# A Mamba-2 scan step whose running sum is split inside its PSUM bank, with the work of four engines in a new order

## The chip, the core and the metric

The kernel runs on one core of one Trainium2 chip, as one launch. The metric is the time of the whole launch on the device, in microseconds (us). TensorE (PE in the profile), VectorE (DVE), ScalarE (ACT), GpSimd (POOL) and SyncE (SP) each run their own instructions in the order in which they are written and meet only at semaphores.

## What is computed

The input is x with 8 sequences of 1024 tokens and 256 features. Two Mamba-2 layers are followed by three blocks of a quantised linear network (the MLP part, which the change leaves alone). Cut to what matters here, a layer is:

```python
h = layernorm(h)
z, xBC, dt = split(h @ in_w.T)                 # 512, 640 and 8 columns
dt  = softplus(dt + dt_bias)
xBC = silu(causal_conv(xBC, 4 taps) + conv_b)  # per channel, along the tokens
x, B, C = split(xBC)                           # 8 heads of 64, and 64 states each
state = exp(dt * A) * state + dt * x (x) B     # token by token
y = state @ C + D * x
y = y * silu(z);  y = y * rsqrt(mean(y * y) + eps) * rms_w
h = h + y @ out_w.T
```

The scan over tokens is computed in chunks of 128 tokens. Within a chunk the product of the decays between tokens j and i is exp(-|cum_i - cum_j|), with cum the running sum of dt * A. The kernel needs cum on the free axis as well as on the partitions, so it splits each fp32 value into three bf16 parts, whose sum is the value, and turns and spreads those with bf16 products.

## The kernel before

One *item* is one chunk of 128 tokens of a group of four sequences. There are 8 chunks and 2 groups, so 16 items in a layer and 32 in all. Every engine has a function `step(n, ...)`, written out by hand, that does its share of item n and of the items after it: the scan and the output of item n, the projections, convolution and `dt` of item n+1, and the norm of item n+2. `over_items` calls it 32 times (the middle twelve of a layer are a loop over two steps, the others are written out). Nothing but that order and the semaphores says when something runs. An instruction that waits holds up all that stands behind it on its engine.

The names that the rest needs, by what they do (q is a half of one sequence's heads, 0 to 7; b is a sequence, 0 to 3; t a quarter of the inner width, 0 to 3; i one of five convolved tiles):

- TensorE: `project_conv(i)`, `project_z(t)` and `project_dt`, six products each (L382, L369); `turn_dt`, `turn_x(b)`, `turn_b`, `turn_u`, transposes; `sum_da`, the running sums, into `front[0]` (L400); `turn_cum`, which transposes the split sum (L408); `decays(q)` (L437); `carry(b)` (L470); `outputs(t)` (L487, L493); `new_state(s)` (L480); `scores` (L425); `result(s)`, the output projection (L530); `square_sums` (L519).
- ScalarE: `raw_conv(i)` moves a projected tile to `xpad` (L658); `silu_conv(i)` (L671); `double_c` issues two DMAs from ScalarE's own queue (L678); `norm`, four instructions (L624); `softplus` (L644 to L648); `exp_decay(q)`, an Abs and an Exp (L696, L698); `exp_carry(b)` (L707); `silu_z(t)` (L692); `square(t)` (L711); `keep_b` (L703).
- GpSimd: `first_tap(i)` (L860), `to_end(b)` (L869), `decay_state` (L876), `layer_norm`, a power (L812) and a product (L824), `gate(t)` (L852), `norm_residual` (L843, L846; in the first layer only), `add_squares` (L837), `second_operands` (L830).
- VectorE: `convolve(i, 0..2)` (L1067, L1070, L1073), which accumulates in the PSUM bank of the projection; `split_sums` (L1005, L1011, L1014); `skip(t)` (L1100); `scale_x(b)` (L1090); `scale_c(b)` (L1095); `weigh(q)` (L1085); `finish(s)` (L1126); `layer_moments`; `decay_operands` (L1033), `first_operands` (L1039), `add_state` (L1110).

A convolved tile passes four engines: `project_conv(i)`, `raw_conv(i)`, `first_tap(i)`, and `convolve(i, 0)` to `convolve(i, 2)`. `turn_cum` waits for the last step of the fifth tile, because it writes the PSUM bank `front[1]` that this tile has used, and for the end of `split_sums`. `turn_u` waits for `silu_z(3)`, which reads the same bank, and `silu_z(3)` waits for `gate(3)`, which reads the buffer that it writes.

Of the kernel before, what the change touches and what calls it, by code (L numbers as in the profile page):

```python
# [174 lines left out]
def mamba_layers(nc, x, h, out, w):  # L175

    with ExitStack() as ctx:
# [49 lines left out]
        rest1, rest2 = sb("rest1", [P, NB, NH]), sb("rest2", [P, NB, NH])  # L227
# [107 lines left out]
        def _(pe):  # L335
# [223 lines left out]
            def step(n, layer, c, p):  # L559
                more, more2 = follows(n, 1), follows(n, 2)  # L560
                decays(n, 4)
                if more:
                    project_conv(n + 1, 0)
                    turn_dt(n + 1)
                if follows_any(n):
# [20 lines left out]
                new_state(n, 0)  # L586
                outputs(n, p, 1)
                if more:
                    project_conv(n + 1, 4)
                    sum_da(n + 1)  # L590
                new_state(n, 1)
                outputs(n, p, 2)
                outputs(n, p, 3)
                if more:
# [5 lines left out]
                    scores(n + 1, 1 - p)  # L600
                    decays(n + 1, 0)
                    decays(n + 1, 1)
                if more2:
                    turn_u(n + 2, p)
# [15 lines left out]
        def _(act):  # L620
# [123 lines left out]
            def step(n, layer, c, p):  # L744
                more, more2 = follows(n, 1), follows(n, 2)
                layer1 = layer_of(n, layer, 1)
                if more:
                    keep_dt(n + 1)
                    raw_conv(n + 1, layer1, 1 - p, 0)
                exp_decay(n, 3)  # L750
# [5 lines left out]
                if more:  # L756
                    raw_conv(n + 1, layer1, 1 - p, 2)
# [3 lines left out]
                exp_decay(n, 7)  # L761
                exp_carry(n, 2)
                exp_carry(n, 3)
                if more:
                    raw_conv(n + 1, layer1, 1 - p, 3)
                    softplus(n + 1)
# [3 lines left out]
                if more:  # L770
# [7 lines left out]
                if more:  # L778
                    keep_halo(n + 1, 1 - p)
                    silu_conv(n + 1, layer1, 1 - p, 3)  # L780
                    silu_conv(n + 1, layer1, 1 - p, 4)
# [1016 lines left out]
```

## Time and profile before

| | us |
|---|---|
| three runs, median (lowest to highest) | 2013.32 (2010.97 to 2015.57) |
| the profiled execution | 2011.51 |
| its span in the profile | 2009.7 |

| engine | busy us | share of the span |
|---|---|---|
| TensorE | 1819.0 | 91% |
| VectorE | 1565.4 | 78% |
| ScalarE | 1258.7 | 63% |
| GpSimd | 1195.9 | 60% |

The launch falls into a ramp of about 100 us, the 16 items of the first layer, the 16 of the second, and from about 1515 us on the MLP part. An item takes about 45 us. The timeline rows give the start of an instruction from the start of the span, its duration, engine, line, operation and tiles, and in brackets how long the engine had been idle before it and who released it. Neighbouring instructions overlap a little, so that the distance of two starts is what an instruction really costs its engine: 0.66 us on VectorE for one shown as 0.75.

### The profile page before, as it was taken

What the parts mean: (1) busy time and instruction counts of PE and PEld (TensorE: products, weight loads), DVE (VectorE), ACT (ScalarE), POOL (GpSimd) and SP (SyncE); (2) the same over time, 40 slices, a digit from 0 to 9 for tenths busy, and PEclk for the clock granted to TensorE, in tenths of its full rate; (3) what the DMA queues carried; (4) which work ended last, traced back from release to release, by engine and by line L of the source; (5) the groups of instructions that cost most, each with busy time, mean ns of one, the idle gap of its engine ahead of it and who ended that gap; (6) DMA issues with size and microseconds to landing.
All of it is one profiled execution on the core that took longest, in us unless ns stands there. A gap on an engine that the chain in (4) does not pass through costs nothing. (4 is left out here: it accounts for less than half of the span.)

```text
span 2009.7 us, 36493 instructions
## 1 busy us (share of the span) xinstructions
PE 1819.0 (91%) x12544; PEld 1366.7 (68%) x12544; DVE 1565.4 (78%) x3311; ACT 1258.7 (63%) x2221; POOL 1195.9 (60%) x1032
## 2 busy tenths in 40 slices
PE   4899999999999999999999999999985698889898
PEld 3566676666676667766676776766764577777776
DVE  4677788887787776877777777777744799999986
ACT  3667666776666776667777676667740355555555
POOL 2466666666666654555555555555550586878785
PEclk9899999999999999999999999999996799999999
DMA  4011111111111111111111111111004201102001
GB/s 139 22 38 38 38 37 39 55 48 37 42 37 37 37 38 38 38 45 59 40 41 37 37 37 37 37 49 45 27 17 146 84 1 62 65 32 95 32 12 43
DMA packets 87271, 91.96 MB, mean 46 GB/s; under 512 B 4928, under 2 KB 82448, under 8 KB 87184
## 3 DMA queue, kind: packets, MB, share of 16 engines
q1 hardware_dynamic: 79360, 79.46, 12.2%
q10 hardware_dynamic: 7824, 11.37, 2.3%
q8 instruction: 51, 0.84, 0.2%
q14 instruction: 36, 0.29, 0.0%
HBM read 57.26 MB, written 25.17 MB: 41 GB/s over the span
## 5 line engine op out<-in xcount | busy, mean ns | idle before, releaser
L860 POOL TENSOR_TENSOR L_xc<-L_xpad,L_vec 128x512 f32<-128x512 f32 x160 | 166.1, 1038 | 318.1 <-ACT L_xpad L658 318.1
L852 POOL TENSOR_TENSOR L_yg<-L_yg,L_sz 128x512 f32<-128x512 f32 x128 | 165.4, 1292 | 159.5 <-DVE L_yg L1100 158.2
L382 PE MATMUL L_front<-L_uhi,L_whi 128*128 128x512 f32 x576 | 250.1, 434 | 9.5 <-DVE L_xc L1073 6.2
L1085 DVE TENSOR_TENSOR L_m<-L_dbank,L_gm 128x512 f32<-128x512 f32 x256 | 173.4, 688 | 101.8 <-ACT L_dbank L698 101.8
L530 PE MATMUL L_mix<-L_wo,L_yg 128*128 128x256 f32 x1024 | 235.4, 384 | 2.6 <-POOL L_yg L852 2.6
L382 PE MATMUL L_front<-L_uhi,L_wlo 128*128 128x512 f32 x576 | 229.2, 398 | 0.0
L382 PE MATMUL L_front<-L_ulo,L_whi 128*128 128x512 f32 x576 | 228.7, 397 | 0.0
L530 PEld LDWEIGHTS L_mix<-L_wo,L_yg 128*128 128x128 f32 x1024 | 191.9, 192 | 27.7 <-POOL L_yg L852 2.8
L658 ACT ACTIVATE L_xpad<-L_front,L_pbias 128x512 f32<-128x512 f32 x160 | 110.1, 688 | 153.1 <-PE L_front L382 153.1
L487 PE MATMUL L_ybank<-L_m,L_dtx 128*64 128x128 f32 x2048 | 158.1, 280 | 33.1 <-DVE L_yg L1100 25.6
L696 ACT ACTIVATE L_dbank<-L_dbank 128x512 f32<-128x512 f32 x256 | 148.7, 581 | 49.7 <-PE L_dbank L437 48.0
L1614 POOL TENSOR_TENSOR M_alo<-M_hT,M_ahi 128x512 fp32r<-128x512 f32 x96 | 125.4, 1310 | 75.0 <-DVE M_ahi L1676 75.0
L487 PEld LDWEIGHTS L_ybank<-L_m,L_dtx 128*64 128x64 f32 x2048 | 113.7, 136 | 81.5 <-issue 33.9
L493 PE MATMUL L_ybank<-L_cs,L_state 64*64 64x128 f32 x2048 | 160.5, 280 | 0.0
L698 ACT ACTIVATE L_dbank<-L_dbank 128x512 f32<-128x512 f32 x256 | 149.0, 582 | 7.5
L382 PEld LDWEIGHTS L_front<-L_uhi,L_whi 128*128 128x128 f32 x576 | 109.6, 190 | 55.3 <-DVE L_xc L1073 20.5
L692 ACT ACTIVATE L_sz<-L_front,L_pbias 128x512 f32<-128x512 f32 x128 | 88.2, 689 | 90.1 <-PE L_front L382 58.7
L1565 ACT ACTIVATE M_g<-M_lin,M_beta,M_gamma 128x512 f32<-128x512 f32 x96 | 73.9, 770 | 111.5 <-PE M_lin L1500 111.5
L869 POOL TENSOR_TENSOR L_wx<-L_dtx,L_decay 128x512 f32<-128x512 f32 x128 | 132.1, 1043 | 8.1 <-DVE L_dtx L1090 7.1
L1621 POOL TENSOR_TENSOR M_alo<-M_g,M_ahi 128x512 fp32r<-128x512 f32 x96 | 134.3, 1418 | 4.2 <-ACT M_ahi L1573 4.1
L1067 DVE SCALAR_TENSOR_TENSOR L_front<-L_front,L_vec,L_xc 128x512 f32<-128x512 f32 x160 | 120.4, 752 | 19.4 <-POOL L_xc L860 19.3
L493 PEld LDWEIGHTS L_ybank<-L_cs,L_state 64*64 64x64 f32 x2048 | 106.4, 132 | 38.4 <-issue 38.4
(176 smaller groups left out, 4949.3 us busy)
## 6 DMA issues: line engine op xcount, KB each, us to landing
h<-L_hres SPq DMA_DIRECT2D x32, 512.0 KB, 3.0
L_hin<-in_x SPq DMA_DIRECT2D x16, 512.0 KB, 4.7
L_hres<-in_x SPq DMA_DIRECT2D x16, 512.0 KB, 3.9
L_cc<-L_xc ACTq DMA_DIRECT2D x64, 128.0 KB, 2.3
L_hin<-h SPq DMA_DIRECT2D x16, 512.0 KB, 4.7
L_hres<-h SPq DMA_DIRECT2D x16, 512.0 KB, 3.8
M_hin<-h SPq DMA_DIRECT2D x16, 512.0 KB, 7.1
M_xin<-in_x SPq DMA_DIRECT2D x16, 512.0 KB, 7.1
```

Source lines behind the costliest of these rows:

```text
L382: last = nc.tensor.matmul(to[:, :], ww[:, kd, tile * P:(tile + 1) * P], a[:, kd, :], start=i == 0, stop=i == len(passes) - 1)
L487: nc.tensor.matmul(ybank[t % 2][half, b * P:(b + 1) * P], dtx[:, b, 2 * t + odd, :], m[:, b, 2 * t + odd, :], start=b == 0, stop=False, sk ...
L493: made = nc.tensor.matmul(ybank[t % 2][half, b * P:(b + 1) * P], state[p][half, b, t, :], cs[half, b, t, :], start=False, stop=True, skip_ ...
L530: last = nc.tensor.matmul(mix[1 - s][:, (b % 2) * DM:(b % 2 + 1) * DM], yg[:, t, b * P:(b + 1) * P], wo[layer][:, t, :], start=t == 0, sto ...
L696: nc.scalar.activation(dbank[q % 2][:, :], dbank[q % 2][:, :], ACT.Abs).then_inc(d_abs, 1)
L698: nc.scalar.activation(dbank[q % 2][:, :], dbank[q % 2][:, :], ACT.Exp, scale=-1.0).then_inc(d_exp, 1)
L852: nc.gpsimd.tensor_tensor(yg[:, t, :], yg[:, t, :], sz[:, t, :], ALU.mult).then_inc(y_gated, 1)
L860: nc.gpsimd.tensor_tensor(xc[p][:, q, :].rearrange("p (b i) -> p b i", b=NB), xpad[:, q, :, 0:P], vector(layer, "conv_w", q * TAPS, 1).uns ...
L869: nc.gpsimd.tensor_tensor(wx[:, b, :, :], dtx[:, b, :, :], decay[p][:, b, :].unsqueeze(2).broadcast_to([P, NH, HD]), ALU.mult).then_inc(wx ...
L1085: nc.vector.tensor_tensor(m[:, b, 4 * half:4 * half + 4, :], dbank[half][:, :].rearrange("p (h i) -> p h i", i=P), gm[:, b, :].unsqueeze(1 ...
L1614: nc.gpsimd.tensor_tensor(alo[u][:, kd, :], hT[u][:, kd, :], ahi[u][:, kd, :].bitcast(F32), ALU.subtract).then_inc(h_lo, 1)
L1621: nc.gpsimd.tensor_tensor(alo[u][:, kd, :], g[u][:, kd, :], ahi[u][:, kd, :].bitcast(F32), ALU.subtract).then_inc(g_lo, 1)
```

## The change

`split_sums` no longer reads the copy of the sums in SBUF. It casts and subtracts from the PSUM bank in which TensorE has left them, and puts the two remainders beside them in that bank (`rest1` and `rest2` in SBUF are gone). The copy to SBUF stays, for ScalarE. The split doesn't wait for it any more, and `project_z(0)`, which overwrites the bank, waits for the end of the split too.

```diff
 def project_z(n, t):
     if t == 0:
         pe.wait_ge(sums_out, n + 1)
+        pe.wait_ge(split, 5 * n + 5)
...
-cum = sums[:, 0, :, :]
-dve.wait_ge(sums_out, n + 1)
+def beside(i):
+    at = (PARTS + i) * NB * NH
+    return front[0][:, at:at + NB * NH].rearrange("p (b h) -> p b h", b=NB)
+
+cum = front[0][:, 0:NB * NH].rearrange("p (b h) -> p b h", b=NB)
+rest1, rest2 = beside(0), beside(1)
 part(0, cum)
```

The rest is order. The products of TensorE are the same ones. Its step begins:

```diff
 # TensorE, step
+project_conv(n + 1, 0)
+turn_x(n, p, 0)
+turn_dt(n + 1)
 decays(n, 4)
-project_conv(n + 1, 0)
-turn_dt(n + 1)
 result(n - 1, layer_of(n, layer, -1), 1)
 project_conv(n + 1, 1)
-turn_x(n, p, 0)
 turn_x(n, p, 1)
+turn_x(n, p, 2)
 decays(n, 5)
 decays(n, 6)
-turn_x(n, p, 2)
 turn_x(n, p, 3)
...
 outputs(n, p, 0)
-new_state(n, 0)
 outputs(n, p, 1)
+outputs(n, p, 2)
 project_conv(n + 1, 4)
 sum_da(n + 1)
+new_state(n, 0)
 new_state(n, 1)
-outputs(n, p, 2)
 outputs(n, p, 3)
```

and further down the first two `decays` of the next item stand ahead of `scores`. On GpSimd:

```diff
 # GpSimd, step
+decay_state(n, p)
 first_tap(n + 1, layer1, 1 - p, 0)
 first_tap(n + 1, layer1, 1 - p, 1)
 to_end(n, p, 0)
-decay_state(n, p)
+first_tap(n + 1, layer1, 1 - p, 2)
 to_end(n, p, 1)
+first_tap(n + 1, layer1, 1 - p, 3)
+layer_norm(n + 2)
 to_end(n, p, 2)
...
+to_end(n, p, 3)
 gate(n, 0)
-to_end(n, p, 3)
-layer_norm(n + 2)
 first_tap(n + 1, layer1, 1 - p, 4)
 gate(n, 1)
```

and `second_operands` stands behind the three `add_squares`. On ScalarE `raw_conv(2)` moves from ahead of `keep_b` to behind `exp_decay(7)`, `softplus` ahead of `raw_conv(3)`, and further down:

```diff
 # ScalarE, step
 silu_conv(n + 1, layer1, 1 - p, 0)
-silu_conv(n + 1, layer1, 1 - p, 1)
-square(n, 0)
-raw_conv(n + 1, layer1, 1 - p, 4)
-double_c(n + 1, 1 - p)
 norm(n + 2, p)
+silu_conv(n + 1, layer1, 1 - p, 1)
+double_c(n + 1, 1 - p)
 silu_conv(n + 1, layer1, 1 - p, 2)
+raw_conv(n + 1, layer1, 1 - p, 4)
+square(n, 0)
 square(n, 1)
+square(n, 2)
```

On VectorE, among others, `scale_x(0)` comes before the convolution of the first tile, `scale_x(2)` and `scale_x(3)` one place earlier each, `finish_dt` behind `skip(0)`, and `skip(1)`, `skip(2)` and `skip(3)` are moved.

How the instructions stand on VectorE around the split, before:

```order
L1073 SCALAR_TENSOR_TENSOR L_xc<-L_xpad,L_vec,L_front 128x512
L99 REGISTER_ALU
L1005 COPY L_sums<-L_front 128x96
L1011 CAST L_cum<-L_sums 128x4x2x8
L1014 TENSOR_TENSOR L_rest<-L_sums,L_cum 128x32
L1011 CAST L_cum<-L_rest 128x4x2x8
L1014 TENSOR_TENSOR L_rest<-L_rest,L_cum 128x32
L1011 CAST L_cum<-L_rest 128x4x2x8
L1066 REGISTER_ALU
L1067 SCALAR_TENSOR_TENSOR L_front<-L_front,L_vec,L_xc 128x512
L1100 SCALAR_TENSOR_TENSOR L_yg<-L_xc,L_vec,L_ybank 128x512
```

and of the changed kernel, whose line numbers are up to five higher:

```order
L1078 SCALAR_TENSOR_TENSOR L_xc<-L_xpad,L_vec,L_front 128x512
L1105 SCALAR_TENSOR_TENSOR L_yg<-L_xc,L_vec,L_ybank 128x512
L99 REGISTER_ALU
L1006 COPY L_sums<-L_front 128x96
L1012 CAST L_cum<-L_front 128x4x2x8
L1015 TENSOR_TENSOR L_front<-L_front,L_cum 128x32
L1012 CAST L_cum<-L_front 128x4x2x8
L1015 TENSOR_TENSOR L_front<-L_front,L_cum 128x32
L1012 CAST L_cum<-L_front 128x4x2x8
L1071 REGISTER_ALU
L1072 SCALAR_TENSOR_TENSOR L_front<-L_front,L_vec,L_xc 128x512
L1105 SCALAR_TENSOR_TENSOR L_yg<-L_xc,L_vec,L_ybank 128x512
```

The casts and remainders read and write `L_front` in place of `L_sums` and `L_rest`, and `skip(1)` (L1100, now L1105) has moved from behind the split to ahead of it.

ScalarE around the move of the fifth convolved tile (L658), the two DMAs (L678) and the norm (L624), before:

```order
L711 ACTIVATE L_sq<-L_yg 128x512
L652 REGISTER_ALU
L658 ACTIVATE L_xpad<-L_front,L_pbias 128x4x128
L674 ISA
L99 REGISTER_ALU
L678 DMA L_cc<-L_xc 64x512 x2
L622 REGISTER_ALU
L624 ACTIVATE L_hin<-L_hin,L_shift,L_rstd 128x256 x4
L670 REGISTER_ALU
L671 ACTIVATE L_xc<-L_xc,L_cbias 128x512
```

and of the changed kernel, from `silu_conv(0)` on:

```order
L672 ACTIVATE L_xc<-L_xc,L_cbias 128x512
L623 REGISTER_ALU
L625 ACTIVATE L_hin<-L_hin,L_shift,L_rstd 128x256 x4
L671 REGISTER_ALU
L672 ACTIVATE L_xc<-L_xc,L_cbias 128x512
L675 ISA
L99 REGISTER_ALU
L679 DMA L_cc<-L_xc 64x512 x2
L671 REGISTER_ALU
L672 ACTIVATE L_xc<-L_xc,L_cbias 128x512
L653 REGISTER_ALU
L659 ACTIVATE L_xpad<-L_front,L_pbias 128x4x128
```

The norm, both DMAs and one more `silu_conv` now stand ahead of `raw_conv(4)`, where it was ahead of all three.

## Rows read from the trace of the kernel before

**Rows 1.** The page, busy time, share of the span and instructions of each engine.
```profile
PE 1819.0 (91%) x12544; PEld 1366.7 (68%) x12544; DVE 1565.4 (78%) x3311; ACT 1258.7 (63%) x2221; POOL 1195.9 (60%) x1032
```

**Rows 2.** Timeline of VectorE, L1115, once per item: items 2, 12, 19, 30.
```profile
203.89 0.16 DVE L1115 TENSOR_SCALAR L_ssq<-L_ybank 128x4 f32<-128x4 f32 x1 [0.27 <-PE L_ybank L519]
...
659.77 0.16 DVE L1115 TENSOR_SCALAR L_ssq<-L_ybank 128x4 f32<-128x4 f32 x1 [0.27 <-PE L_ybank L519]
...
937.50 0.16 DVE L1115 TENSOR_SCALAR L_ssq<-L_ybank 128x4 f32<-128x4 f32 x1 [0.72 <-PE L_ybank L519]
...
1431.65 0.16 DVE L1115 TENSOR_SCALAR L_ssq<-L_ybank 128x4 f32<-128x4 f32 x1 [0.72 <-PE L_ybank L519]
```

**Rows 3.** Timeline of TensorE over one item of the first layer.
```profile
607.99 1.09 PE L342 MATMUL L_front<-L_kept,L_hin 128*128 128x128 f32 x8 [0.59 <-ACT L_sz L692]
...
615.43 0.39 PE L437 MATMUL L_dbank<-L_dmov,L_dstat 64*128 64x512 bf16 x1
...
620.95 0.58 PE L382 MATMUL L_front<-L_uhi,L_whi 128*128 128x512 f32 x1
...
622.54 0.60 PE L450 MATMUL L_mix<-L_kept,L_xc 128*128 128x128 f32 x4
623.82 0.66 PE L450 MATMUL L_mix<-L_kept,L_xc 128*128 128x128 f32 x4 [0.69 <-DVE L_hres L1126]
...
630.70 0.73 PE L470 MATMUL L_mix<-L_dmov,L_sel 64*128 64x512 bf16 x4
631.77 0.44 PE L487 MATMUL L_ybank<-L_m,L_dtx 128*64 128x128 f32 x4 [0.34 <-DVE L_m L1085]
...
643.54 1.09 PE L487 MATMUL L_ybank<-L_m,L_dtx 128*64 128x128 f32 x16 [0.76 <-DVE L_yg L1100]
...
645.60 0.28 PE L408 MATMUL L_front<-L_identb,L_cum 128*128 128x128 bf16 x2
```

**Rows 4.** The same view, `turn_u` of an item of the second layer.
```profile
1156.13 1.09 PE L342 MATMUL L_front<-L_kept,L_hin 128*128 128x128 f32 x8
```

**Rows 5.** Timeline of ScalarE (ACTq: its queue issuing DMAs), the same item.
```profile
631.34 1.07 ACT L707 ACTIVATE L_mix<-L_mix 128x512 f32<-128x512 f32 x2 [0.65 <-PE L_mix L470]
632.31 0.69 ACT L658 ACTIVATE L_xpad<-L_front,L_pbias 128x512 f32<-128x512 f32 x1
632.88 0.24 ACT L644 ACTIVATE L_dtabs<-L_dtraw 128x32 f32<-128x32 f32 x1
...
634.94 1.28 ACT L671 ACT_TABLE_LOAD   x1
...
639.54 1.12 ACTq L678 DMA_DIRECT2D L_cc<-L_xc  x2
640.77 2.08 ACT L624 ACTIVATE L_hin<-L_hin,L_shift,L_rstd 128x256 f32<-128x256 f32 x4 [0.76 <-POOL L_shift L824]
642.75 0.70 ACT L671 ACTIVATE L_xc<-L_xc,L_cbias 128x512 f32<-128x512 f32 x1
```

**Rows 6.** Timeline of GpSimd, the same item.
```profile
638.86 1.00 POOL L812 TENSOR_TENSOR L_rstd<-L_var,L_power 128x4 f32<-128x4 f32 x1
640.03 0.20 POOL L824 TENSOR_TENSOR L_shift<-L_mom,L_rstd 128x4 f32<-128x4 f32 x1 [0.17 <-POOL L_rstd L812]
640.18 1.04 POOL L860 TENSOR_TENSOR L_xc<-L_xpad,L_vec 128x512 f32<-128x512 f32 x1
```

**Rows 7.** Timeline of VectorE, the same item.
```profile
620.25 0.18 DVE L992 TENSOR_TENSOR L_dtraw<-L_front,L_dtb 128x32 f32<-128x32 f32 x1
...
640.37 0.91 DVE L1011 CAST L_cum<-L_sums 128x64 bf16<-128x64 f32 x1
...
641.53 0.20 DVE L1011 CAST L_cum<-L_rest 128x64 bf16<-128x64 f32 x1
...
642.09 0.75 DVE L1067 SCALAR_TENSOR_TENSOR L_front<-L_front,L_vec,L_xc 128x512 f32<-128x512 f32 x1
642.75 0.74 DVE L1100 SCALAR_TENSOR_TENSOR L_yg<-L_xc,L_vec,L_ybank 128x512 f32<-128x512 f32 x1
```

More of the change, by code:

```diff
@@ L560, in step @@
                 more, more2 = follows(n, 1), follows(n, 2)
-                decays(n, 4)
                 if more:
                     project_conv(n + 1, 0)
+                turn_x(n, p, 0)
+                if more:
                     turn_dt(n + 1)
+                decays(n, 4)
                 if follows_any(n):
@@ L748, in step @@
                     keep_dt(n + 1)
+                exp_decay(n, 3)
+                if more:
                     raw_conv(n + 1, layer1, 1 - p, 0)
-                exp_decay(n, 3)
                 exp_decay(n, 4)
@@ L755, in step @@
                 exp_decay(n, 6)
-                if more:
-                    raw_conv(n + 1, layer1, 1 - p, 2)
                 keep_b(n)
@@ L761, in step @@
                 exp_decay(n, 7)
+                if more:
+                    raw_conv(n + 1, layer1, 1 - p, 2)
                 exp_carry(n, 2)
@@ L775, in step @@
                 if more:
+                    silu_conv(n + 1, layer1, 1 - p, 1)
+                    double_c(n + 1, 1 - p)
                     silu_conv(n + 1, layer1, 1 - p, 2)
+                    raw_conv(n + 1, layer1, 1 - p, 4)
+                square(n, 0)
                 square(n, 1)
[L778 to L781, printed above, removed]
-                    silu_z(n + 1, layer1, 0)
                 square(n, 2)
                 if more:
+                    silu_conv(n + 1, layer1, 1 - p, 3)
+                    silu_z(n + 1, layer1, 0)
+                    keep_halo(n + 1, 1 - p)
                     silu_z(n + 1, layer1, 1)
+                    silu_conv(n + 1, layer1, 1 - p, 4)
                     silu_z(n + 1, layer1, 2)
                     silu_z(n + 1, layer1, 3)
+                    exp_decay(n + 1, 0)
                 square(n, 3)
                 if more:
-                    exp_decay(n + 1, 0)
                     exp_decay(n + 1, 1)
@@ L1169, in step @@
                 if more:
+                    set_halo(n + 1, 1 - p)
+                weigh(n, 3)
+                scale_x(n, p, 0)
+                if more:
+                    bias_dt(n + 1, layer1)
                     convolve(n + 1, layer1, 1 - p, 0, 0)
-                    bias_dt(n + 1, layer1)
-                    convolve(n + 1, layer1, 1 - p, 0, 1)
-                weigh(n, 3)
                 weigh(n, 4)
                 if more:
-                    convolve(n + 1, layer1, 1 - p, 0, 2)
+                    convolve(n + 1, layer1, 1 - p, 0, 1)
                 if follows_any(n):
                     finish(n - 1, layer_of(n, layer, -1), None, 1 - p, 1)
-                scale_x(n, p, 0)
+                if more:
+                    convolve(n + 1, layer1, 1 - p, 0, 2)
                 scale_x(n, p, 1)
+                scale_x(n, p, 2)
                 if more:
                     convolve(n + 1, layer1, 1 - p, 1, 0)
-                scale_x(n, p, 2)
+                scale_x(n, p, 3)
                 if more:
                     convolve(n + 1, layer1, 1 - p, 1, 1)
-                scale_x(n, p, 3)
                 weigh(n, 5)
@@ L1205, in step @@
                     convolve(n + 1, layer1, 1 - p, 3, 2)
+                skip(n, layer, p, 1)
+                if more:
                     split_sums(n + 1)
                     convolve(n + 1, layer1, 1 - p, 4, 0)
-                skip(n, layer, p, 1)
+                skip(n, layer, p, 2)
                 if more:
                     convolve(n + 1, layer1, 1 - p, 4, 1)
-                skip(n, layer, p, 2)
-                if more:
                     convolve(n + 1, layer1, 1 - p, 4, 2)
                     decay_operands(n + 1)
-                skip(n, layer, p, 3)
+                    first_operands(n + 1)
                 add_state(n, p, 0)
-                if more:
-                    first_operands(n + 1)
                 add_state(n, p, 1)
@@ L1221, in step @@
                     clear_halo(n, p)
+                skip(n, layer, p, 3)
                 if more:
```

33 lines of the change are left out of this document (15 added, 18 removed).

## Prediction

> **What bounds the kernel now.** The page gives TensorE 91% of the span [rows 1], so I first ask how often it waits. The change only touches the two layers, so I need the length of an item: one row of VectorE stands once in each. In the first layer ten items lie between 203.89 and 659.77, which is 45.59 us each. In the second, eleven lie between 937.50 and 1431.65, 44.92 us each [rows 2].
>
> The timeline of TensorE over one item then shows where it is idle [rows 3]: 0.59 us before `turn_u` (released by `silu_z(3)`), 0.69 before `turn_x(1)` (`finish`), 0.34 before `outputs(0)` (`weigh(7)`), 0.76 before `outputs(3)` (`skip(1)`). In the second layer the wait before `turn_u` is absent [rows 4], and 45.59 - 44.92 = 0.67 is about its size. So four waits of 2.4 us are shown. With what hides between the products I put the loss at 3 us an item, and TensorE without waits at 42.3 to 42.6. With some 15 items' distance in each layer, all of it is worth at most 30 x 2.8, about 84 us. TensorE's work is unchanged: the change can only bring what its waits lose, and an order is as good as the latest thing that it makes TensorE wait for. The question is which wait takes the place of the four.
>
> **The split.** In the item shown, its first cast takes 0.91 us, the later ones of the same size 0.20 [rows 7]. The long one started at 640.37 and ended at 641.28, while GpSimd ran `first_tap(4)` from 640.18 to 641.22 [rows 6]: it was held until GpSimd was through. A read from PSUM of 128x32 took 0.18 us [rows 7], so the five new steps should be no dearer than the old, and the first loses its wait for the copy too, 0.1 to 0.2 us. The split gets up to 0.8 us shorter, in the ramp once as well.
> The Trainium skill (SBUF — State Buffer, the section on the two sides of SBUF) says that VectorE in a two-port mode and GpSimd hold one pair of ports in turn, and "VectorE: DVE Perf Modes" (why PSUM operands drop a tier) that a PSUM operand excludes that mode. The row of 0.91 us agrees. The same page's cost table speaks against the change: 120 fixed cycles from PSUM in place of 58 from SBUF, which is 5 x 0.065 = 0.3 us more by my estimate. The row of 0.18 us does not show it. With it the split would save 0.5 us, not 0.8.
>
> **The first part of an item, by the new order.** I walk with starts of the old item, whose step begins at 615.43 [rows 3].
> - TensorE. Ahead of `project_conv(1)` now also stands `turn_x(0)`, 0.43 to 0.47 us, and `project_conv(0)` follows `project_dt` 0.1 us sooner. So `project_conv(1)` starts at 620.95 + 0.35 = 621.3 and ends 1.59 later (622.54 - 620.95), at 622.9. `finish` let `turn_x(1)` start at 623.82, so it ran from about 622.9, behind `convolve(0, 2)`. It now stands ahead of that and is done at about 622.8, so the 0.69 us before `turn_x(1)` goes to nearly nothing.
> - The second tile: `raw_conv(1)` 623.1 to 623.8 (0.69 [rows 5]), `first_tap(1)` to 624.9 (1.04 [rows 6]), then on VectorE `convolve(1, 0)`, `scale_x(3)`, `convolve(1, 1)`, `weigh(5)`, `convolve(1, 2)`, at 0.66 a convolution and 0.60 a product, done at 628.2. `project_conv(3)` waits for it: 628.3 to 629.9. `outputs(0)` follows at about 630.7, 1.1 us sooner than before, and its wait of 0.34 shrinks to 0.2.
> - `carry(2)` from 629.9; ScalarE gets it 0.64 later (630.70 to 631.34), so `exp_carry(2)` and `(3)` run 630.5 to 631.5 (0.97 for both).
> - Now the tail on ScalarE. `softplus` costs 634.94 - 632.88 = 2.06: to 633.6. `raw_conv(3)`, now behind it, to 634.2 (0.57 of ScalarE's time, done at 634.3). The table load 1.29 and `silu_conv(0)` 0.66: 636.1. Meanwhile GpSimd: `first_tap(3)` 634.3 to 635.4, then `layer_norm`, 1.37 us from the start of the power to the end of the product (638.86 to 640.23 [rows 6]), shift ready at 636.7. So `norm` starts at 636.8 and takes 1.98 (642.75 - 640.77). `silu_conv(1)` at 638.8. Then `double_c`: its two DMAs block ScalarE's queue, 1.12 us from 639.54 on. The norm behind them started at 640.77, though the shift that the row names was there at 640.23. It was the DMA issue that held it. So from `silu_conv(1)` to `silu_conv(2)` it is 0.22 + 1.12 + 0.11 = 1.45 and not 0.66: 640.2. `raw_conv(4)` 640.9 to 641.6, where it ended at 640.0 before.
> - `first_tap(4)` to 642.7, `convolve(4, 0)`, `skip(2)`, `convolve(4, 1)` at 0.66 a start, `convolve(4, 2)` behind them with 0.13 more for its dependence, done at 645.6. `turn_cum` waits for that.
>
> So `turn_cum` comes at about 645.65, against 645.60 before. TensorE has done all else that stands ahead of it by 643.8: the four waits of before shrink to some 0.4 us, and a new one of 1.8 us stands before `turn_cum`, for the fifth tile. The split ends at about 641.4, while VectorE waits for `first_tap(4)` until 642.7. GpSimd would not even have held it there, because it waits for the same tile. So I cost the 0.8 us of the split at nothing in steady items: the cover is the late `raw_conv(4)`, and without it the 0.8 us would count.
>
> **The second part.** From `turn_cum` to the next step nothing is added. `second_operands` moves behind the squares and fills the time in which GpSimd waits for the mean square. `gate(3)` still comes behind `norm_residual`. In the first layer `skip(3)` is later (650.4), `gate(3)` ends at 651.9, `silu_z(3)` at 652.7, and `turn_u`, with both `decays` and `scores` ahead, is due at 652.9: the wait of 0.6 to 0.7 us goes. In the second layer there was none.
>
> **Sum.** First layer: 15 x (0.05 - 0.67) = -9.3 us. Second layer: 15 x 0.05 = +0.75. Ramp: -0.8, where nothing covers the split. Together -9.4 us, on 2011.5 of the profiled execution or 2013.3 of the median, which lies 1.8 above it: 2003.9, say 2003.5.
>
> **Bounds.** Each 0.1 us by which `turn_cum` shifts is 3 us. The walk goes through some 25 hand-overs of 0.04 to 0.09 us, and I trust its end to about 0.4 us either way: 1991.5 to 2015.5. The price of a PSUM remainder is bounded by 0.18 (the nearest row) and 0.26 a step; neither end shows while the cover holds.
>
> **The rivals.**
> 1. *The tail is earlier than I think.* If `norm` finds its shift ready or the DMA issue costs ScalarE less in its new place, `raw_conv(4)` comes sooner and the split's own gain begins to count. For it: TensorE is ready 1.8 us before. Against: each link has a row. At 0.7 us sooner it is 2003.5 - 21 = 1982.5; the limit, with that wait all gone, is 2003.5 - 54 = 1949.5.
> 2. *No gain.* The tail is 0.2 to 0.45 us later than walked, so that the two ends cancel: 2009.5 to 2017.
> 3. *Slower, by the queue ahead of `raw_conv(4)`.* `raw_conv(2)` now waits behind `exp_decay(7)`, and GpSimd does `first_tap(2)`, `to_end(1)`, `first_tap(3)` before `layer_norm`, whose shift `norm` needs, behind which `raw_conv(4)` stands. It is a chain through three engines without slack. It decides from 0.45 us on; at 0.8 us it is 2003.5 + 24 = 2027.5. For it: the idle time is now all in one place, and every hand-over adds. Against: by the walk GpSimd stands idle for 1.6 us ahead of `first_tap(4)`, so its own work is not what is late.
> 4. *The split from PSUM is held by GpSimd all the same.* Then only the ramp's 0.8 us is lost: 2004.3. It is inside the forecast.
>
> **Chances.** Forecast (with 4) 0.40, rival 1 0.16, rival 2 0.22, rival 3 0.22. A run of this kernel can tell about 0.2%, 4 us, from no change. The forecast and rival 1 are faster by more than that: 0.56. Same 0.22, slower 0.22. The range leaves out the ends of rivals 1 and 3: 1984 to 2021.
>
> **What would show it.** Right: in the profile after, one wait of about 1.8 us before the transposes of the split sum, released by the last convolution step. No wait before the transposes of u in the first layer, and items of about 45.0 us in both layers. ScalarE's idle time before the norm named as GpSimd's shift, and the move of the fifth tile starting about 4.8 us before that wait ends. All three casts of the split 0.2 us or so. Wrong: items of unlike length in the two layers, a wait of TensorE in another place above 0.5 us, or VectorE never idle ahead of the fifth tile.

## The result and the profile after

| | before | after |
|---|---|---|
| median of four runs each, side by side, us | 2013.98 (2010.97 to 2015.57) | 1981.19 (1979.39 to 1981.88) |
| span of the profiled execution | 2009.7 | 1980.0 |

The ratio of the times is 0.9838, with a 95% interval of 0.9821 to 0.9855. The gain is 33 us where 10 were forecast, and the time lies 2.8 us below the range.

The page of the changed kernel gives the busy times that answer to [rows 1]. TensorE does the same work in a shorter span, VectorE is 30 us less busy:

```profile
span 1980.0 us, 36525 instructions
PE 1819.1 (92%) x12544; PEld 1380.2 (70%) x12544; DVE 1534.9 (78%) x3311; ACT 1260.0 (64%) x2221; POOL 1189.5 (60%) x1032
```

The row of VectorE that stands once in each item is now L1120 (L1115 in [rows 2]). Two neighbouring items of the first layer, two of the second, and the last two items of the scan:

```profile
593.00 0.16 DVE L1120 TENSOR_SCALAR L_ssq<-L_ybank 128x4 f32<-128x4 f32 x1 [0.67 <-PE L_ybank L519]
636.93 0.16 DVE L1120 TENSOR_SCALAR L_ssq<-L_ybank 128x4 f32<-128x4 f32 x1 [0.68 <-PE L_ybank L519]
...
1351.39 0.16 DVE L1120 TENSOR_SCALAR L_ssq<-L_ybank 128x4 f32<-128x4 f32 x1 [0.80 <-PE L_ybank L519]
1395.31 0.16 DVE L1120 TENSOR_SCALAR L_ssq<-L_ybank 128x4 f32<-128x4 f32 x1 [0.80 <-PE L_ybank L519]
...
1438.42 0.16 DVE L1120 TENSOR_SCALAR L_ssq<-L_ybank 128x4 f32<-128x4 f32 x1 [1.46 <-PE L_ybank L519]
1479.58 0.16 DVE L1120 TENSOR_SCALAR L_ssq<-L_ybank 128x4 f32<-128x4 f32 x1 [7.63 <-PE L_ybank L519]
```

Inside a layer, items take 43.93 us in both layers, against 45.59 and 44.92 before. The last item is the exception: 41.16 us, where it took 34.57 before. The same rows, followed through all 32 items in both kernels, give this account:

| stretch | before | after | change |
|---|---|---|---|
| start to the first item's row | 112.83 | 109.83 | -3.0 |
| 14 items, first layer | 638.24 | 615.73 | -22.5 |
| the item with the change of layer | 52.52 | 55.07 | +2.55 |
| 15 items, second layer | 671.85 | 657.79 | -14.1 |
| last item | 34.57 | 41.16 | +6.6 |
| from there to the end | 499.69 | 500.42 | +0.7 |
| span | 2009.7 | 1980.0 | -29.7 |

So the loop gave 36.6 us (the forecast was 8.6), and the change of layer and the last item took 9 back. Of the -3.0 at the start I make nothing: two kernels below whose code is the same up to there (the one with the last item's order and the one with products added in waits) have that row at 111.86 and 111.37, and over all kernels here it lies between 109.8 and 113.2.

TensorE's waits in an item answer to [rows 3]. These are the starts at `turn_x(1)`, `outputs(0)`, `turn_cum` and `turn_u`:

```profile
601.83 1.03 PE L450 MATMUL L_mix<-L_kept,L_xc 128*128 128x128 f32 x8
609.85 0.44 PE L487 MATMUL L_ybank<-L_m,L_dtx 128*64 128x128 f32 x4 [0.27 <-DVE L_m L1090]
623.53 0.28 PE L407 MATMUL L_front<-L_identb,L_cum 128*128 128x128 bf16 x2 [0.62 <-DVE L_xc L1078]
630.83 1.09 PE L341 MATMUL L_front<-L_kept,L_hin 128*128 128x128 f32 x8
```

Of the four waits one of 0.27 is left. The new one, before `turn_cum` and released by the last convolution step, is where the prediction put it, but 0.62 us long and not 1.8. From 594 to 632 us no other wait of TensorE is named.

### The profile page after: what moved, and what is told of

Its sections match the earlier page's. It is cut to its first block and busy times, and to the rows that moved or that the text cites. A ratio compares the mean times of both kernels' runs of the same rounds, so it can differ in the third digit from the quotient of the medians.

```text
span 1980.0 us, 36525 instructions
## 1 busy us (share of the span) xinstructions
PE 1819.1 (92%) x12544; PEld 1380.2 (70%) x12544; DVE 1534.9 (78%) x3311; ACT 1260.0 (64%) x2221; POOL 1189.5 (60%) x1032
## 5 line engine op out<-in xcount | busy, mean ns | idle before, releaser
L837 POOL TENSOR_TENSOR L_sq<-L_sq 128x512 f32<-128x512 f32 x96 | 122.0, 1270 | 55.6 <-ACT L_sq L712 52.5
L712 ACT ACTIVATE L_sq<-L_yg 128x512 f32<-128x512 f32 x128 | 80.0, 625 | 110.7 <-POOL L_yg L852 110.7
L487 PEld LDWEIGHTS L_ybank<-L_m,L_dtx 128*64 128x64 f32 x2048 | 111.8, 137 | 53.2 <-issue 42.6
```

Of the source, the lines that this page charges most:

```text
L487: nc.tensor.matmul(ybank[t % 2][half, b * P:(b + 1) * P], dtx[:, b, 2 * t + odd, :], m[:, b, 2 * t + odd, :], start=b == 0, stop=False, sk ...
```

## Experiments

All kernels were timed side by side with the kernel of before, whose medians were 2014.3 to 2014.9 us in the three groups of runs and 2014.5 beside the last. "The row" is the one that stands once in an item.

### The two halves of the change, each alone

The new order on all engines, with the split as it was:

```diff
+        rest1, rest2 = sb("rest1", [P, NB, NH]), sb("rest2", [P, NB, NH])
...
-                    pe.wait_ge(split, 5 * n + 5)
...
-                cum = front[0][:, 0:NB * NH].rearrange("p (b h) -> p b h", b=NB)
-                rest1, rest2 = beside(0), beside(1)
+                cum = sums[:, 0, :, :]
+                dve.wait_ge(sums_out, n + 1)
```

> The new order on all four engines, but the split reads the SBUF copy and keeps its remainders in SBUF, as before. Theory A (in the changed kernel the split stands on the path: it ends at 620.55 and convolve(4, 0) starts at that instant, first_tap(4) having ended at 620.47): the first cast is held again until first_tap(4) ends and the later steps follow, so each of 30 items gets 0.9 to 1.1 us longer, 2008 to 2014 us. Rival B (the cover of the prediction holds and the split costs nothing in steady items): 1981 to 1985 us.

Measured: 2067.29 us, ratio 1.0262 (1.0245 to 1.028). Both expectations are off by 50 us and more: the new order alone is the slowest kernel of all. VectorE and GpSimd in one of its items:

```profile
654.25 1.04 POOL L860 TENSOR_TENSOR L_xc<-L_xpad,L_vec 128x512 f32<-128x512 f32 x1 [0.74 <-ACT L_xpad L659]
654.48 0.86 DVE L1012 CAST L_cum<-L_sums 128x64 bf16<-128x64 f32 x1
655.24 1.28 POOL L852 TENSOR_TENSOR L_yg<-L_yg,L_sz 128x512 f32<-128x512 f32 x1
655.37 1.20 DVE L1015 TENSOR_TENSOR L_rest<-L_sums,L_cum 128x32 f32<-128x32 f32 x1
...
656.83 0.19 DVE L1015 TENSOR_TENSOR L_rest<-L_rest,L_cum 128x32 f32<-128x32 f32 x1
...
660.14 0.28 PE L408 MATMUL L_front<-L_identb,L_cum 128*128 128x128 bf16 x2 [2.39 <-DVE L_xc L1074]
```

The first cast ends when `first_tap(4)` ends, as before. What is new is the line below: the first remainder, which reads two SBUF tiles, takes 1.20 us where the next one takes 0.19. `gate(1)` started 0.13 us ahead of it, and it ends when `gate(1)` does. In the new order GpSimd runs these two without a gap, so VectorE is held twice, and TensorE waits 2.39 us before `turn_cum`.

The order of before, with the split in PSUM:

```diff
-        rest1, rest2 = sb("rest1", [P, NB, NH]), sb("rest2", [P, NB, NH])
...
+                    pe.wait_ge(split, 5 * n + 5)
...
-                cum = sums[:, 0, :, :]
-                dve.wait_ge(sums_out, n + 1)
...
+                cum = front[0][:, 0:NB * NH].rearrange("p (b h) -> p b h", b=NB)
+                rest1, rest2 = beside(0), beside(1)
```

> The order of before with the split in PSUM. Before, convolve(4, 0) and skip(1) stood behind the split, and TensorE waited 0.76 us for skip(1) before outputs(3). Theory A (the split is worth its 0.9 us wherever it has no cover): that wait goes, 0.75 to 0.85 us in each of 30 items, 1986 to 1992 us. Rival B (the gain is the order's, the split is hidden by other work of VectorE): 2009 to 2013 us.

Measured: 1990.17 us, ratio 0.9878 (0.9861 to 0.9894), with items of 44.78 us in the first layer (about 44.84 and 44.71 in turn) and 44.13 in the second: 0.8 us less in each layer. The first cast is 0.7 us shorter and starts sooner, because it no longer waits for the copy; in the old order all of the 0.8 us counts:

```profile
678.17 1.09 PE L487 MATMUL L_ybank<-L_m,L_dtx 128*64 128x128 f32 x16
...
688.27 0.98 PE L341 MATMUL L_front<-L_kept,L_hin 128*128 128x128 f32 x7 [0.59 <-ACT L_sz L692]
```

The first line is `outputs(3)`, which waited 0.76 us for `skip(1)` in [rows 3] and no longer waits. The wait before `turn_u` is still there.

Together the two runs say that the parts can't be priced one by one. The split is worth 25 us in the old order and 86 in the new (2067.3 to 1981.2). The order costs 52 us with the old split and gains 9 with the new.

### Which reads of SBUF are held

The changed kernel, with one operand moved: the first cast reads the copy in SBUF again.

```diff
-                part(0, cum)
+                dve.wait_ge(sums_out, n + 1)
+                part(0, sums[:, 0, :, :])
```

> The changed kernel, but the first cast of the split reads the copy in SBUF; the remainders and the later casts stay in PSUM. One question: is a single cast of 128x32 from SBUF, in a place where GpSimd runs without a gap, enough to lose time? A (the cast is held for as long as GpSimd's first_tap(4) lasts): in the changed kernel the first cast starts at 619.44 and first_tap(4) ends at 620.47, the split 620.63; held, the cast ends at 620.67 and the split at 621.5, 0.9 us later, which stands on the path: 30 x 0.9 = 27 us, 2003 to 2011 us, the cast at 0.9 to 1.2 us. B (only the remainder with two SBUF inputs is held): the cast stays at 0.2 to 0.3 us, 1980 to 1984 us.

Measured: 2000.93 us, ratio 0.9937 (0.992 to 0.9953), items of 44.80 us. A holds in the item (0.87 us longer, the cast at 0.89). The total is 2 us below its range: four of the items at the start and the end of a layer are not longer, and the last item takes 39.7 us here and the change of layer 53.4, against 41.16 and 55.07.

```profile
629.07 0.89 DVE L1012 CAST L_cum<-L_sums 128x64 bf16<-128x64 f32 x1
```

The changed kernel with both remainders written to SBUF (and read there):

```diff
+        rest1, rest2 = sb("rest1", [P, NB, NH]), sb("rest2", [P, NB, NH])
...
-                rest1, rest2 = beside(0), beside(1)
```

> The changed kernel, but both remainders are written to SBUF: the first cast and the first remainder still read the sum in PSUM, the second cast reads SBUF, the second remainder has two SBUF inputs, the third cast reads SBUF. A (both kinds are held): the second cast starts at about 619.9 on the changed kernel's scale and is held until first_tap(4) ends at 620.47, and the second remainder is then held by gate(1), which starts at 620.43 and takes 1.28, until 621.7; the split ends near 622.1, 1.4 us later than now: 30 x 1.4 = 42 us, 2015 to 2030 us, one remainder of about 1.1 us and the other of 0.2. B (as in the run with everything in SBUF, 2067 us, because the gates and skips then fall behind each other as well): above 2045 us. C (neither is held): 1980 to 1984 us.

Measured: 2044.82 us, ratio 1.0157 (1.014 to 1.0174).

```profile
645.55 1.04 POOL L861 TENSOR_TENSOR L_xc<-L_xpad,L_vec 128x512 f32<-128x512 f32 x1 [0.75 <-ACT L_xpad L660]
646.54 1.28 POOL L853 TENSOR_TENSOR L_yg<-L_yg,L_sz 128x512 f32<-128x512 f32 x1
...
645.56 0.21 DVE L1013 CAST L_cum<-L_front 128x64 bf16<-128x64 f32 x1
645.80 0.19 DVE L1016 TENSOR_TENSOR L_rest<-L_front,L_cum 128x32 f32<-128x32 f32 x1
646.03 0.61 DVE L1013 CAST L_cum<-L_rest 128x64 bf16<-128x64 f32 x1
646.67 1.20 DVE L1016 TENSOR_TENSOR L_rest<-L_rest,L_cum 128x32 f32<-128x32 f32 x1
```

Here one kernel shows the four cases side by side. A cast that reads PSUM and a remainder with one SBUF input run at 0.2 us in the middle of `first_tap(4)`. A cast from SBUF waits for its end (0.61), and a remainder with two SBUF inputs waits for the end of `gate(1)` (1.20). The Trainium skill (SBUF — State Buffer, "Who interferes with whom") states just this: VectorE in a two-port mode, or with two SBUF inputs while GpSimd reads SBUF, waits for a GpSimd instruction that started sooner, and whichever starts first holds the shared ports to its end. The trace agrees, at the 0.61 and 1.20 above; that the held cast is in a two-port mode no row names.

The split ends 1.4 us later than in the changed kernel, as A says, and the total is 15 us above A and just under B. The items come in two lengths in turn, 45.28 and 46.85 us. The 45.28 are A (43.93 + 1.35). The other 1.57 us of every second item was not in any expectation. Busy time by stretch of that kernel, and its `turn_cum`, show where it is (stretch, its length, busy time of PE, PEld, DVE, ACT and POOL, then TensorE's granted clock, the share of the DMA engines, GB/s; of the clock 1.00 is the upper of two levels, 2.4 GHz, and 0.50 the lower, 1.2 GHz, so I read a value between as a stretch with both):

```profile
160.00:700.00 540.00, 511.34 (x3630) 374.54 (x3629) 420.59 (x843) 368.10 (x654) 339.99 (x282) 0.98 0.14 41
...
650.00:655.00 5.00, 4.01 (x13) 3.19 (x14) 4.38 (x8) 2.08 (x4) 4.83 (x3) 0.72 0.00 0
```

```profile
650.99 0.28 PE L408 MATMUL L_front<-L_identb,L_cum 128*128 128x128 bf16 x2 [1.97 <-DVE L_xc L1074]
```

The clock is 0.98 from 800 to 1390 too, and 1.00 in both stretches in the kernels before and after. In slices of 5 us it is 0.72 from 650 to 655, right behind `turn_cum` and its wait of 1.97 us, and 1.00 in the slices behind the same place in the item ahead of it. So I filled the wait: six products whose results nobody reads, into banks that are free there.

```diff
                 outputs(n, p, 3)
                 if more:
+                    for i in range(6):
+                        nc.tensor.matmul(dbank[i % 2][:, :], dstat[0:ROWS, 0, :], dmov[0:ROWS, 0, 0:4, :], start=True, stop=True)
                     turn_cum(n + 1)
```

> The kernel with both remainders in SBUF (2044.8 us, items of 45.28 and 46.85 us in turn, TensorE idle 2.0 us ahead of the transposes of the sum), with six products of 512 bf16 columns added in that wait; nobody reads their results. In that kernel every second item shows a lower granted clock behind the wait (0.72 from 650 to 655), the others 1.00. A (the hold makes an item 1.4 us longer and TensorE's clock, which falls behind the longer wait, the other 1.57 us of every second item): the clock stays at 1.00 in the loop, all items take 45.2 to 45.4 us, 30 x 0.78 = 23 us less: 2018 to 2025 us. B (the long items have another cause, a queue that is late every second time): 2042 to 2048 us and items of two lengths as before.

Measured: 2021.91 us, ratio 1.0036 (1.0023 to 1.0049), with items of 45.28 us throughout. A holds: 23 us of that kernel were TensorE's clock behind the wait and not the hold of the split.

```profile
160.00:700.00 540.00, 528.08 (x3751) 381.16 (x3749) 424.91 (x848) 376.13 (x667) 347.33 (x287) 1.00 0.14 41
```

The same account fits the kernel with the order alone, where it was not tested. Its shorter items take 45.73 us, which is 43.93 and the 1.8 by which its wait is longer, and two of three take 47.28, which is 1.55 more; its granted clock from 160 to 700 is 0.97.

### The DMA issue on ScalarE's queue

In the new order `double_c` stands behind `norm` and `silu_conv(1)`. ScalarE (ACTq is its queue issuing a DMA) in an item of the changed kernel:

```profile
615.48 0.60 ACT L625 ACTIVATE L_hin<-L_hin,L_shift,L_rstd 128x256 f32<-128x256 f32 x1 [0.45 <-POOL L_shift L824]
615.79 0.47 ACTq L679 DMA_DIRECT2D L_cc<-L_xc  x1
615.99 0.59 ACT L625 ACTIVATE L_hin<-L_hin,L_shift,L_rstd 128x256 f32<-128x256 f32 x1
616.29 0.62 ACTq L679 DMA_DIRECT2D L_cc<-L_xc  x1
616.48 1.07 ACT L625 ACTIVATE L_hin<-L_hin,L_shift,L_rstd 128x256 f32<-128x256 f32 x2
617.46 1.32 ACT L672 ACTIVATE L_xc<-L_xc,L_cbias 128x512 f32<-128x512 f32 x2
618.69 0.66 ACT L659 ACTIVATE L_xpad<-L_front,L_pbias 128x512 f32<-128x512 f32 x1
```

The two DMAs are written behind `silu_conv(1)`, which starts at 617.46, and are issued from 615.79 on, while the norm ahead of them still runs. Then `silu_conv(1)` and `(2)` follow each other without a gap. The theory: the queue runs ahead of the instructions in execution, so a DMA costs its issue time only where the engine has nothing queued that it can run meanwhile. To take the run-ahead away, ScalarE waits for the norm's own end before it issues:

```diff
-            def double_c(n, p):
+            def double_c(n, p, hold=False):
                 act.wait_ge(conved, QCONV * n + 1)
+                if hold:
+                    act.wait_ge(ln_done, n + 2)
...
-                    double_c(n + 1, 1 - p)
+                    double_c(n + 1, 1 - p, hold=more2)
```

> The changed kernel, with one wait more on ScalarE: the two DMAs of double_c are not issued before the norm's last instruction has ended. Theory A (the changed kernel gains over the walk because ScalarE's queue issues the DMAs while four norm instructions stand queued; held back they cost the 0.8 us that the walk had charged): raw_conv(4) starts 0.75 us later, 2001 to 2006 us, about the predicted number. Rival B (the walk's surplus lay elsewhere, the DMA issue costs ScalarE nothing in either place): 1981 to 1984 us.

Measured: 2007.5 us, ratio 0.9962 (0.9948 to 0.9976), items of 44.85 us in both layers, against 45.0 in the prediction.

```profile
674.93 0.71 ACT L672 ACTIVATE L_xc<-L_xc,L_cbias 128x512 f32<-128x512 f32 x1
675.25 1.12 ACTq L681 DMA_DIRECT2D L_cc<-L_xc  x2
676.48 0.72 ACT L672 ACTIVATE L_xc<-L_xc,L_cbias 128x512 f32<-128x512 f32 x1 [0.83 <-ACT L_xc L672]
...
681.91 0.28 PE L407 MATMUL L_front<-L_identb,L_cum 128*128 128x128 bf16 x2 [1.62 <-DVE L_xc L1080]
```

From `silu_conv(1)` to `(2)` it is 1.55 us (the walk had 1.45), and `turn_cum` waits 1.62 us (the walk had 1.8). This kernel does what the prediction forecast for the changed one. The added wait is over at 675.03, with the norm, and `silu_conv(1)` starts 1.98 us after the norm in both kernels, so the wait holds the issue and little else.

### The last item

There TensorE has nothing of a next item to do. First its order: in the changed kernel `turn_x(0)` stands ahead of `result(1)`, and waits 2.35 us for `finish` with nothing behind it to fill the time.

```diff
                 if more:
                     project_conv(n + 1, 0)
-                turn_x(n, p, 0)
-                if more:
+                    turn_x(n, p, 0)
                     turn_dt(n + 1)
...
                     project_conv(n + 1, 1)
+                else:
+                    turn_x(n, p, 0)
```

> The changed kernel, only in the very last item TensorE does decays(4) and the output projection of the item before ahead of turn_x(0), as it did before. Theory A (in that item nothing stands ahead of turn_x(0), TensorE is idle for 2.35 us waiting for finish and then runs at half clock for some 20 us): 5 to 6.5 us less, 1974.5 to 1976.5 us. Rival B (the half clock there comes anyway, since it was there before for a shorter time): 1 to 2.5 us less, 1979 to 1980.5 us.

Measured: 1980.28 us, ratio 0.9829 (0.9812 to 0.9845). The last item is 39.31 us instead of 41.16, and the total is in B's range: TensorE then waits 2.17 us before `turn_x(1)`, and its clock falls later but just as low, to 0.50 from 1455 to 1460. The change of layer took 53.44 us in this execution and 55.07 in that of the changed kernel, with the same code there, so 1.6 of the +2.55 above vary from one execution to the next.

Then products that nobody reads were put into TensorE's waits, 34 in the last item and 10 at the change of layer:

```diff
+            def ballast(n, count):
+                pe.wait_ge(gm_done, n + 1)
+                for _ in range(count):
+                    nc.tensor.matmul(ybank[0][:, 0:NB * ROWS], identb[:, :], cum3[:, :, :].rearrange("p b r -> p (b r)"), start=True, stop=True)
...
+                else:
+                    ballast(n, 16)
                 turn_x(n, p, 0)
```

> The changed kernel with products added on TensorE whose results nobody reads, only where it waits: 16, 8, 6 and 4 products of 256 bf16 columns ahead of the transposes of x(0), x(1) and of the second and third carry product of the last item, and 10 ahead of the bias sums at the change of layer. They test what the 8.5 us cost by which the change of layer and the last item are slower than in the kernel of before. A (it is TensorE's clock, which falls to half there behind the waits): with the clock kept up the last item's output product takes 3.7 us instead of 5.77, its output stage 1.5 us less, the bias sums 5.2 instead of 7.44 and the first projection of the new layer 1.4 instead of 2.6: 5 to 8 us less, 1972 to 1976 us. B (the clock falls all the same, or the path there is VectorE's and GpSimd's): the added products only take room, 1980 to 1984 us.

Measured: 1974.29 us, ratio 0.9803 (0.9787 to 0.9819). The last item is 34.77 us, 6.4 less, and as long as before the change. First the busy time by stretch of the changed kernel there, then of this one:

```profile
1440.00:1445.00 5.00, 4.26 (x11) 3.00 (x12) 2.57 (x5) 1.16 (x2) 2.60 (x2) 0.50 0.01 3
...
1455.00:1460.00 5.00, 4.32 (x29) 1.94 (x30) 2.57 (x4) 1.64 (x3) 0.00 (x0) 0.67 0.00 0
```

```profile
1440.00:1445.00 5.00, 4.64 (x23) 3.76 (x24) 2.19 (x5) 1.16 (x2) 2.22 (x2) 1.00 0.00 0
...
1455.00:1460.00 5.00, 5.00 (x74) 3.71 (x72) 1.50 (x2) 0.63 (x1) 1.72 (x2) 1.00 0.02 3
```

The granted clock is 1.00 where it was 0.50 and 0.67, and the output product takes 3.72 us instead of 5.77. At the change of layer the ten products did nothing: 53.41 us, against 53.44 in the kernel above, and the clock falls to 0.50 there in this kernel too, over the bias sums (36 single-column entries in the trace). It falls to 0.50 over them in the kernel before as well; what the rest of the difference there is, no run here tests.

### What is still to be had

VectorE's `skip(2)` stands between two steps of the convolution for which `turn_cum` waits. It was moved behind them:

```diff
                     convolve(n + 1, layer1, 1 - p, 4, 0)
-                skip(n, layer, p, 2)
-                if more:
                     convolve(n + 1, layer1, 1 - p, 4, 1)
                     convolve(n + 1, layer1, 1 - p, 4, 2)
+                skip(n, layer, p, 2)
+                if more:
```

> The changed kernel with skip(2) on VectorE moved from between the first and second step of the fifth tile's convolution to behind the third. In the changed kernel TensorE waits 0.62 us before the transposes of the sum for that third step, and skip(2) takes 0.66 of VectorE's time ahead of it. A (that step is the only thing that TensorE waits for there): it comes 0.6 us sooner in every item, the wait goes to under 0.1, items of 43.3 to 43.4 us in both layers, 30 x 0.6 = 18 us: 1962 to 1966 us. B (gate(2) on GpSimd, which waits for skip(2), comes 0.6 us later and with it gate(3), silu_z(3) and the transposes of u): the first layer gains nothing and waits before the transposes of u instead, only the second layer gains: 1970 to 1974 us. C (VectorE is late for something else after it): 1978 us and up.

Measured: 1996.11 us, ratio 0.9912 (0.9896 to 0.9929), items of 44.4 us in the first layer and 44.3 in the second: 15 us slower than the changed kernel. By its number it is C, by its cause none of the three. The wait before `turn_cum` is gone, but:

```profile
631.49 1.30 POOL L852 TENSOR_TENSOR L_yg<-L_yg,L_sz 128x512 f32<-128x512 f32 x1 [0.94 <-DVE L_yg L1105]
632.81 0.63 ACT L712 ACTIVATE L_sq<-L_yg 128x512 f32<-128x512 f32 x1 [2.57 <-POOL L_yg L852]
...
633.97 0.67 ACT L693 ACTIVATE L_sz<-L_front,L_pbias 128x512 f32<-128x512 f32 x1
...
634.68 0.50 PE L381 MATMUL L_front<-L_uhi,L_whi 128*128 128x512 f32 x1 [0.66 <-ACT L_sz L693]
```

`gate(2)` waits for `skip(2)`, `square(2)` on ScalarE for `gate(2)`, behind it in the queue stand `silu_conv(3)` and `silu_z(0)`, and TensorE's `project_z(2)` waits for the bank that `silu_z(0)` reads. So `square(2)` was moved as well:

```diff
-                square(n, 2)
                 if more:
                     silu_conv(n + 1, layer1, 1 - p, 3)
                     silu_z(n + 1, layer1, 0)
+                square(n, 2)
+                if more:
```

> The changed kernel with skip(2) behind the fifth tile's convolution, as in the run that was slower (1996.1 us, items of 44.35), and square(2) on ScalarE moved from ahead of silu_conv(3) and silu_z(0) to behind silu_z(0). In that run gate(2) came late behind skip(2) (631.49 to 632.77), square(2) waited for it until 632.81, silu_z(0) behind it until 633.97, and TensorE 0.66 us for silu_z(0) before project_z(2). A (that queue is the whole cause): silu_z(0) needs only its product, 1.5 us after the transposes, and the wait before project_z(2) goes; the second layer gets items of 43.3 to 43.4 us and gains 15 x 0.55 = 8 us on the changed kernel; the first layer gains 0 to 0.2 an item, because gate(3), still behind norm_residual, holds silu_z(3) and so the transposes of u: 1969 to 1974 us. B (gate(2) coming late is itself the loss): 1985 us and up.

Measured: 1981.33 us, ratio 0.9831 (0.9816 to 0.9846), between A and B. The second layer does as A says, 43.40 us an item. The first layer does not: 44.4 us, where I had 43.7 to 43.9, with a new wait before `turn_u`:

```profile
588.28 2.34 POOL L844 TENSOR_TENSOR L_hres<-L_hres,L_mean 128x1024 f32<-128x1024 f32 x1
...
592.56 1.26 POOL L853 TENSOR_TENSOR L_yg<-L_yg,L_sz 128x512 f32<-128x512 f32 x1
593.91 0.69 ACT L693 ACTIVATE L_sz<-L_front,L_pbias 128x512 f32<-128x512 f32 x1 [2.21 <-POOL L_yg L853]
594.66 1.09 PE L341 MATMUL L_front<-L_kept,L_hin 128*128 128x128 f32 x8 [0.86 <-ACT L_sz L693]
```

What I had left out: a late `gate(2)` also pushes `norm_residual` back (it starts at 588.28), and `gate(3)`, at 592.56, stands behind that. The next two kernels were written, with their expectations, before this result was known. In the first of them `gate(3)` was put between the two halves of `norm_residual` in the first layer:

```diff
                                         ALU.subtract).then_inc(res_normed, 1)
+                if between is not None:
+                    between()
                 pool.wait_ge(res_normed, 2 * n + 1)
...
-                    norm_residual(n + 1, c + p, 1 - p)
-                gate(n, 3)
+                    norm_residual(n + 1, c + p, 1 - p, lambda: gate(n, 3))
+                else:
+                    gate(n, 3)
```

> The previous one, and in the first layer gate(3) on GpSimd stands between the two halves of norm_residual instead of behind them. A (in the first layer gate(3) is what silu_z(3) and the transposes of u wait for): silu_z(3) comes 1 us or more sooner, no wait before the transposes of u, the first layer's items come down to 43.3 to 43.5 us as the second's: 15 x 0.5 = 7 us less than the previous run, 1962 to 1967 us. B (not held there): the same as the previous run within 2 us.

Measured: 1964.66 us, ratio 0.9754 (0.9739 to 0.9769), items of 43.40 us in both layers. A holds, and the gain on the previous kernel is 16.7 us and not 7, since that one had lost in the first layer. It is 16.5 us below the changed kernel. The second of them has, besides, the added products of the last item and of the change of layer:

> The previous one with the added products of the run that kept TensorE's clock up in the last item (that run: 1974.3 us, last item 34.8 us instead of 41.2). A (the two gains are independent: one in the loop, one in the last item): 6 to 7 us less than the previous run, 1955 to 1961 us, last item of 34.5 to 35.5 us. B (the last item starts in another phase of TensorE's clock and keeps it without them): within 3 us of the previous run.

Measured: 1963.24 us in five runs, ratio 0.9744 (0.9731 to 0.9757). By the total it is B (1.4 us less); the last item takes 38.77 us instead of 41.31, where A had 34.5 to 35.5. Counted from the first added product, TensorE's starts in it are those of the kernel of 1974.29 us up to the output stage, but the granted clock is 0.81 and 0.51 in the slices from 1435 to 1445, where it was 1.00 in that one. Why the same added products held the clock in one kernel and not in the other stays open.

## Why the prediction was wrong

**Direction and form: right.** The change is faster. The waits before `turn_x(1)`, `outputs(3)` and, in the first layer, `turn_u` are gone. One of 0.27 is left before `outputs(0)` (0.2 in the text). The new wait stands before `turn_cum` and for the fifth tile's last step. The items are equally long in both layers. The norm starts when GpSimd's shift is there, within 0.2 us of the walk, whose `project_dt` lies 21.13 us later than this item's. The move of the fifth tile starts 4.84 us before the wait for it ends, where 4.8 was forecast. Of the signs of being wrong that the text names one came: VectorE goes from the split straight into the fifth tile, with no idle time between them.

**The step that failed: the DMA issue in the tail on ScalarE.** The text says that the two DMAs "block ScalarE's queue" and puts 1.45 us from `silu_conv(1)` to `silu_conv(2)`. It was 0.66. The row that it rests on [rows 5] is true, and a wait of the norm behind the DMAs did come from them. But in that place the queue had just waited for TensorE before `raw_conv(4)`, and issued only once that had begun, 0.22 us later:

```profile
639.32 0.69 ACT L658 ACTIVATE L_xpad<-L_front,L_pbias 128x512 f32<-128x512 f32 x1 [0.76 <-PE L_front L382]
```
In the new place four instructions of the norm are queued ahead, and the issue fits under them. `raw_conv(4)` started at 618.69 where the walk (less 21.13) had 619.77; `turn_cum` at 623.53 where it had 624.52. That is 1.0 us an item, 0.8 of it the DMA issue, which is about 24 of the 28 us by which the loop is shorter than forecast. With the issue held by a wait the kernel takes 2007.5 us, near the 2003.5 predicted; there the DMAs cost 0.9 us an item, a little more than the 0.8 of the walk.

**Rival 1 had it.** It names "the DMA issue costs ScalarE less in its new place", and at 0.7 us it gives 1982.5 us. The mechanism was on the list; what was wrong is the 0.16 for it and the 0.40 for the forecast. The evidence against was one row from a place with other neighbours. A bound from both sides was due there: with the issue at nothing the same sum gives 2003.5 - 30 x 0.79 = 1979.8 us, below the 1984 at which the range began.

**The split at nothing: wrong, as a consequence.** In the new order, with the DMAs hidden, the split ends at 620.63 and `first_tap(4)` at 620.47:

```profile
619.43 1.04 POOL L860 TENSOR_TENSOR L_xc<-L_xpad,L_vec 128x512 f32<-128x512 f32 x1 [0.73 <-ACT L_xpad L659]
619.44 0.21 DVE L1012 CAST L_cum<-L_front 128x64 bf16<-128x64 f32 x1
...
620.41 0.22 DVE L1012 CAST L_cum<-L_front 128x64 bf16<-128x64 f32 x1
...
620.55 0.75 DVE L1072 SCALAR_TENSOR_TENSOR L_front<-L_front,L_vec,L_xc 128x512 f32<-128x512 f32 x1
```

The cover is gone, and the text did say that the 0.8 us would count then. It also said that GpSimd "would not even have held it there". In the kernel with the DMA issue held, both are so: GpSimd is idle for 1.69 us before `first_tap(4)`, four of the five steps of the split have started and ended by then, and VectorE waits 0.90 us for that tile (the split in SBUF under a held issue was not run). In the changed kernel neither is. With the split in SBUF it was held by two instructions, not one, and the price was 86 us, part of it, by the account above, TensorE's clock behind the longer wait. The hold was read from the cast alone; the remainder with two SBUF inputs was never held in the kernel before, because nothing followed `first_tap(4)` closely there. The same hold shows what the change is: an order in which GpSimd works without a gap beside the split, and a split that doesn't mind.

**PSUM as a source: right.** The casts take 0.21 and 0.22 us and the remainders 0.20, against 0.20 and 0.19 from SBUF; the second to the fourth step together take 0.73 us from start to start and 0.68 before. The extra fixed cost of PSUM that the Trainium skill gives (VectorE: DVE Perf Modes, the errata-adjusted cycle table; 0.065 us a step by my estimate) is about 0.02 here.

**The ends: not in the prediction.** The last item and the change of layer cost 9 us more than before. In the last item it is TensorE's clock behind new waits, shown by filling them (-6.4 us). Of the change of layer, 1.6 us vary from one execution to the next and the rest is open. The two ends hide a part of the gain.

**TensorE without waits: put too low.** The text has 42.3 to 42.6 us an item. In the kernel with items of 43.40 us TensorE shows one wait of 0.27 us in an item and is busy for 533.6 of the 540 us from 160 to 700, from which I estimate some 43 us.

## What to carry to other kernels

A DMA issue on an engine's queue has no price of its own: look at what is ahead of it in the queue. Behind instructions that are ready it was hidden, behind a wait it cost 0.9 us of its 1.12, and that wait alone was worth 26 us here. An order and the operands that run in it are one choice: check every VectorE instruction with SBUF sources against what GpSimd will do beside it in the new order, above all two-input ones. And before a step is moved back to free the critical engine, follow its result through all queues that wait for it; it took three edits on three engines until moving `skip(2)` paid (1996.1, 1981.3, 1964.7 us).

## What the runs showed of the hardware

- A 128x32 subtraction with two SBUF inputs took 1.20 us where GpSimd had started a 128x512 product 0.13 us sooner, and 0.19 otherwise; with one input in PSUM it took 0.19 to 0.20 in the middle of a GpSimd product.
- ScalarE's queue issued the first of two DMAs 1.7 us before the instruction written ahead of it began. They took 0.47 and 0.62 us of the queue, and none of the engine's. Behind a wait for the norm's end they took 1.12 us of the queue, and the next instruction came 0.9 us later.
- Waits of TensorE of 1.97 us and 2.39 us in the loop were followed by a lower granted clock in every second item and in two of three, which took 1.55 to 1.57 us longer; in the kernel with a wait of 1.62 us the items are all alike. Filling the wait of 1.97 us with products gave the 1.57 us back.
- In the last item the same added products kept the clock at 1.00 in one kernel and not in another whose items are 0.5 us shorter; what decides that, these runs don't tell.
